# Cross attention in another order: the next pair's scores and the last pair's output ahead of a pair's values

## What is computed

```python
def reference(...):
    x = x + 0.5 * _L0_ffn_ref(_layernorm(x), ...)      # x: (4, 2048, 256)
    x = x + _L0_attn_ref(_layernorm(x), ...)
    x = x + 0.5 * _L0_ffn_ref(_layernorm(x), ...)
    return x

def _L0_attn_ref(hidden_states, Wq, Wk, Wv, Wo, W1, b1, W2, b2):
    initial = hidden_states[:, :256]
    remaining = hidden_states[:, 256:]
    comp = relu(initial @ W1 + b1) @ W2 + b2
    comp = comp.reshape(B, 64, 4, D).mean(axis=2)       # 64 keys
    remaining_out = _cross_attn(remaining, comp, Wq, Wk, Wv, Wo)
    initial_out = _causal_self_attn(initial, Wq, Wk, Wv, Wo)
    return concatenate([initial_out, remaining_out], axis=1)

def _cross_attn(seq, ctx, Wq, Wk, Wv, Wo):              # 16 heads of 16
    scores = einsum('bqhd,bkhd->bhqk', Q, K) * scale
    probs = softmax(scores, axis=-1)
    out = einsum('bhqk,bkhd->bqhd', probs, V).reshape(B, S, 256)
    return out @ Wo
```

## Time and profile before

| | |
|---|---|
| median of 3 runs | 1761.8 us (1752.37 to 1766.24) |
| profiled execution, span | 1859.2 us |
| mean granted clock of TensorE | 0.876 of 2.4 GHz |
| TensorE, busy | 1470.4 us, 79% |
| VectorE, busy | 1063.1 us, 57% |
| ScalarE, busy | 614.9 us, 33% |
| GpSimd, busy | 842.1 us, 45% |

### The profile page before, as it was taken

The page is one execution under the profiler, slowest core; times in us unless marked ns, Lnnn a source line. Parts: engine busy times, 40 slices in busy tenths (PEclk is TensorE's granted clock), DMA queues, the critical chain, the costliest instruction groups (busy, mean ns, idle before and its releaser), DMA issues. The chain is left out here.

```text
span 1859.2 us, 35672 instructions
## 1 busy us (share of the span) xinstructions
PE 1470.4 (79%) x11274; PEld 1241.7 (67%) x11275; DVE 1063.1 (57%) x3355; ACT 614.9 (33%) x1254; POOL 842.1 (45%) x1060
## 2 busy tenths in 40 slices
PE   3988976999987889788787889699783649699760
PEld 3888876988875558655685668588552439598650
DVE  4688745644436676757765775243654666473332
ACT  2333312444433333243223332244331213244220
POOL 4545795555553200221183007655424535656636
PEclk9999987999997999899887989799777769799785
DMA  3643323556553113312231022356423551365555
GB/s 110 197 142 110 99 72 103 167 162 154 162 158 111 46 61 97 111 38 69 69 118 59 24 75 72 112 166 159 137 71 95 159 164 58 108 156 168 159 163 181
DMA packets 175219, 215.72 MB, mean 116 GB/s; under 512 B 18800, under 2 KB 156144, under 8 KB 175088
## 3 DMA queue, kind: packets, MB, share of 16 engines
q0 software_dynamic: 28416, 77.63, 16.3%
q1 hardware_dynamic: 100976, 92.32, 15.6%
q10 hardware_dynamic: 45696, 44.05, 7.3%
HBM read 119.56 MB, written 94.37 MB: 115 GB/s over the span
## 5 line engine op out<-in xcount | busy, mean ns | idle before, releaser
L778 POOL DMA_INDIRECT rows_and_results<-normalised_by_token,rows_of_slots x336 | 319.6, 951 | 227.8 <-PE bank L1608 143.2
L718 POOL DMA_INDIRECT gathered_results<-slot_results,slot x128 | 122.2, 955 | 301.4 <-DVE combined_rows L1447 229.6
L1388 DVE TENSOR_TENSOR rows_transposed_low<-bank,rows_transposed_high 128x512 fp32r<-128x512 f32 x168 | 116.0, 691 | 245.2 <-ACT rows_transposed_high L897 174.7
L1619 PE MATMUL bank<-expert_gate_up_high,rows_transposed_high 128*128 x672 | 212.9, 317 | 29.8 <-DVE rows_transposed_low L1388 14.8
L1620 PE MATMUL bank<-expert_gate_up_low,rows_transposed_high 128*128 x672 | 196.0, 292 | 3.6 <-issue 3.3
L1621 PE MATMUL bank<-expert_gate_up_high,rows_transposed_low 128*128 x672 | 194.7, 290 | 0.0
L1775 PE MATMUL bank<-expert_down,hidden_work 128*128 x672 | 187.8, 404 | 2.8 <-DVE hidden_work L1404 2.3
L793 POOL TENSOR_SCALAR keys_high<-iota,place_in_page_of_choice 128x128 fp32r<-128x128 f32 x96 | 57.7, 601 | 288.2 <-issue 225.2
L1619 PEld LDWEIGHTS bank<-expert_gate_up_high,rows_transposed_high 128*128 128x128 f32 x672 | 133.9, 199 | 46.3 <-issue 44.7
L1619 PE MATMUL bank<-rows_transposed_high,shared_gate_up_high 128*128 128x256 f32 x512 | 160.9, 314 | 1.1 <-DVE hidden_work L1121 1.1
L1620 PE MATMUL bank<-rows_transposed_low,shared_gate_up_high 128*128 128x256 f32 x512 | 154.5, 302 | 0.0
(11 more groups left out here) (275 smaller groups left out, 3700.3 us busy)
## 6 DMA issues: line engine op xcount, KB each, us to landing
slot_results<-rows_and_results ACTq DMA_DIRECT2D x168, 256.0 KB
partial_sums<-rows_and_results SPq DMA_DIRECT2D x96, 256.0 KB, 2.1
rows_and_results<-partial_sums SPq DMA_DIRECT2D x72, 256.0 KB, 2.7
normalised_by_token<-normalised_rows SPq DMA_DIRECT2D x64, 256.0 KB, 3.2
rows_and_results<-in_L_attn_hidden_states SPq DMA_DIRECT2D x32, 256.0 KB, 3.1
normalised_rows<-partial_sums SPq DMA_DIRECT2D x24, 256.0 KB
out<-normalised_rows SPq DMA_DIRECT2D x24, 256.0 KB
rows_and_results<-normalised_by_token,rows_of_slots POOLq DMA_INDIRECT x336
```

Of the source, the lines that this page charges most:

```text
L718: gp.indirect_dma_start(into[:, t, k, :], None, ys[part], bass.IndirectOffsetOnAxis(ap=slot[:, b, k, 2 * i + t:2 * i + t + 1], axis=0))\
L778: gp.indirect_dma_start(rows[:, i % NS, t, :], None, norm_d, bass.IndirectOffsetOnAxis(ap=listed[:, page:page + 1], axis=0))\
L1388: dve.tensor_tensor(flat(xt_l[:, k]), bank[k][:], flat(xt_h[:, k]).bitcast(F32), ALU.subtract)\
L1619: pe.matmul(out_, lh, rh, start=first, stop=False)
```

## The change

In each turn of the loop, TensorE now does the turn of the maxima and the turned scores of i, the rows of i+2, then the output of pair i-1 (before: i-2, at the turn's begin), the scores of i+1, the values of i, and the queries of i+2 at the end (before: i+1, ahead of the maxima). The queries of pair 2 stand ahead of the loop, which is the same place as before. VectorE adds pair i-1 behind the low part of the queries (before: i-2, behind the maxima). ScalarE copies the maxima ahead of the queries. All outputs but that of pair 7 go to bank 1, which holds the queries too: so the output waits for the low part of the queries of the pair two ahead of it, and queries from pair 3 on wait for the addition of the pair three back. The turn of the maxima no longer waits for an addition.

```diff
         def output_bank(ph, i):
-            return bank[int(i == PB - 2 and ph["opens"] is not None)]
+            return bank[int(i < PB - 1)]
...
                 for i in range(1, PB):
-                    if i + 1 < PB:
-                        queries_high(i + 1)
                     if i == PB - 1 and ph["opens"]:
                         token_apply(ph["opens"], 0)
                         token_apply(ph["opens"], 1)
                     maxima(i)
+                    if i + 1 < PB:
+                        queries_high(i + 1)
                     exps(i)
...
                 for i in range(1, PB):
                     maxima(i)
-                    if i > 1:
-                        add(i - 2)
                     norm(i - 1)
                     if i + 1 < PB:
                         queries_low(i + 1)
+                    add(i - 1)
                     if i + 2 < PB:
                         low(i + 2)
...
-                add(PB - 2)
                 norm(PB - 1)
...
                 rows_turned(ph, 2)
+                queries(ph, 2)
                 for i in range(1, PB):
-                    if i > 1:
-                        output(ph, i - 2)
-                    if i + 1 < PB:
-                        queries(ph, i + 1)
                     turn_maxima(ph["a"] + i)
                     scores_turned(ph, i)
                     if i + 2 < PB:
                         rows_turned(ph, i + 2)
+                    output(ph, i - 1)
                     if i == PB - 1 and ph["opens"]:
                         token_turn(ph["opens"], 0)
-                    values(ph, i)
                     if i + 1 < PB:
                         scores(ph, i + 1)
-                output(ph, PB - 2)
+                    values(ph, i)
+                    if i + 2 < PB:
+                        queries(ph, i + 2)
...
                 pe.wait_ge(a_ql.sem, a_ql.freed(a, 1))
+                if i > 2:
+                    pe.wait_ge(a_out.sem, a_out.done(a - 3))
...
                 pe.wait_ge(a_norm.sem, a_norm.done(a))
-                if i + 3 < PB:
-                    pe.wait_ge(a_low.sem, a_low.done(a + 3))
+                if i + 2 < PB:
+                    pe.wait_ge(a_ql.sem, a_ql.done(a + 2))
...
                     pe.wait_ge(x_mx.sem, x_mx.done(a - a // PB - 1))
-                    pe.wait_ge(a_out.sem, a_out.freed(a, 2))
```

## The result

The changed kernel takes 1767.3 us (median of 20 runs, 1758.67 to 1777.6), the kernel before 1760.1 beside it (20 runs, 1752.37 to 1768.64). The ratio of paired runs is 1.004, with a 95% interval of 1.0022 to 1.0057: 4 to 10 us slower. That is within 1%, in the range, and 4 us above the point. The direction is that of the small loss in the sum (+1.5), and the loss is larger than the sum had it.

The account below looks back on a forecast made before the run. Bound: the chain between TensorE, VectorE and ScalarE in the attention stages; TensorE's gain is given back by VectorE's wait for the output. Bounds -2 and +5, middle +1.5: 1761.8 + 1.5 = 1763 us, range 1746 to 1777.

Parts of the forecast that it names:

- the small loss in the sum: Three attention stages at -2 to +5 us, batch 3's stage at 0; middle +1.5, so 1761.8 becomes 1763.
- The case: Whole kernel: nothing measurable changes, chance 0.78, own range 1752 to 1773 us; 0.82 for staying within 1%.
- Neither rival: Faster, VectorE not held: 1744 us, chance 0.13. Slower, TensorE at 1.2 GHz in each pair: 1784 us, chance 0.09.
- The plain pair: A pair without extra VectorE work, such as pair 5: 8.9 us, before 9.88.
- TensorE's loop: Scores 0.60, values 2.45, queries 1.75, turn to exp 1.93, exps 2.07, handing over 0.1: 8.90 us per plain pair.
- scores within 0.2 of the last exp's end: Mark of a right prediction: in the new timeline the next scores start within 0.2 us of the last exp's end.
- The pairs with more work: Pairs where VectorE also combines, does layer norm or statistics: pair 2 11.1, pair 3 14.0, pair 6 12.3 us.
- The tail: Stage end, from pair 7's maxima to the last addition: 17.49 us before, 16.8 at full clock, 18.4 at low clock.
- the pause at pair 7: TensorE waits 4.6 us for pair 7's maxima, before 1.84; low clock assumed behind it, tail 0.9 longer.
- the base: Stage 1 of the one profiled execution before, 83.03 us, taken for all three attention stages.
- the middle of the bounds: Three attention stages together: bounds -2 and +5 us, their middle +1.5 taken as the forecast change.
- the faster rival: Additions don't stall VectorE, so all six gaps gain 1.0: 6 us per stage, 18 in three, 1744; chance 0.13.

Follow-up runs that it names:

- e1: The kernel before, unchanged, profiled once more beside the changed kernel: 1771.51 us in the one run, span 1769.8.
- e5: Changed kernel plus eleven unread matmuls on TensorE ahead of the turn of the maxima of pairs 4 and 7: 1766.1 us, ratio to before 1.0017.
- e3: Changed kernel with VectorE's addition of pair i-2 back directly behind the maxima, TensorE keeping the new order: 1787.1 us, ratio to before 1.0128.
- e4: Changed kernel with VectorE's combining, statistics and low part of the rows put ahead of the addition: 1750.9 us, ratio to before 0.9936.
- e8: Changed kernel with VectorE's other work ahead of the addition, plus six and eight unread matmuls at pairs 4 and 7: 1743.4 us, ratio to before 0.9891.

## Why the prediction was right, and where it was not

**The case and the sign were right.** The main forecast was that the time does not move by more than about 1%, because VectorE's wait for the output gives back what TensorE's chain gains. It held. Neither rival came: VectorE was held at every addition (18.5 us in the stage), so the gain of 18 us is not there; the clock did not fall in the plain pairs 1 and 5, which take 8.90 to 8.91 in all three stages. From the maxima of pair 1 to those of pair 7 it is 66.0 to 66.2, well within the 3 us around 65.5 that the prediction allowed, and the stage of batch 3 is not clearly shorter (134.6 against 134.5 and 135.2).

**The plain pair: 8.9 forecast, 8.91 measured, but partly for a wrong reason.** I had TensorE's loop at 8.90 and VectorE's at 8.69, and took the first as the bound. It is the other way round: two errors, one in each sum, left the number right, and that is luck.

- TensorE's terms were too large. The values with all exps ready take 1.86 (642.65 to 644.51), not 2.45; I had scaled 24 of 32 passes that themselves waited for exps. The queries take 1.53 (644.51 to 646.04), not 1.75, and from turn to exp it is 1.73 (646.04 to 647.77), not 1.93. So that loop sums to 7.9.
- VectorE's had one term too small: from the queries' low part to the addition it is 642.15 - 639.32 = 2.83, where the sum had 0.60 + 2.0. The 0.23 between them is the time from the low part's end to the output's start (640.15). The loop is 2.39 (maxima) + 2.48 (norm) + 2.83 + 0.61 (addition) + 0.60 (low part) = 8.91, the whole distance.
- The mark "scores within 0.2 of the last exp's end" failed accordingly: the exps end at 640.94, and the scores start at 642.05, 1.1 later. The output stands between them on TensorE's queue, and it waited 0.72 for the queries' low part. I had put the output beside the exps, but it is VectorE that sets its start.

The timeline behind the turn, from which 1.73 comes:

```profile
646.04 0.38 PE L1606 MATMUL bank<-identity,score_maxima 128*128 128x128 f32 x2
...
647.77 2.07 ACT L971 ACTIVATE raw_weights<-bank 128x512 f32<-128x512 f32 x4 [0.45 <-PE bank L1917]
```

**The pairs with more work were right in kind, each 0.2 too short.** Pair 2: 11.1 forecast, 11.27 measured. Pair 3: 14.0, and 14.18 and 14.19 in stages 2 and 3 (15.26 in stage 1, with its slow output). Against the 14.46 of its base the prediction took pair 3 for a gain; against the 13.5 to 13.8 of e1 it is a loss. Pair 6: 12.3, and 12.54. The mis-sized 2.6 that is 2.83 is the same in each of them. Pair 4: 10.4, and 10.26 and 10.22 (9.30 in stage 1, where the clock was rising again when the output began, which took 1.98, against 2.94 in stage 2). The maxima of pairs 6 and 7, timeline of VectorE after:

```profile
643.36 2.47 DVE L1486 TENSOR_REDUCE score_maxima<-bank 128x8 f32<-128x512 f32 x4
...
655.90 2.48 DVE L1486 TENSOR_REDUCE score_maxima<-bank 128x8 f32<-128x512 f32 x4
```

**The tail and the clock were right.** 4.6 forecast for the pause at pair 7, 4.95 measured; the clock fell, and the tail is 17.60, 18.15 and 18.13, between the 16.8 at full and the 18.4 at low clock. In e5, with the pauses filled, it is 17.02, so that the fall costs 0.6 to 1.1 here, and at pair 4 the 9.3 to 10.3 become 8.92. The Trainium skill (TensorE: Matmul & The Clock Gate, "HAM oscillation — how this bites in real kernels") says that a pause inside a loop brings the half rate back each time; the windows agree, with 0.50 and 0.55 behind the two long pauses in after and 1.00 in e5. The pause of 2.05 at pair 3 had no forecast, and it cost 1.1 in one stage of three.

**The shared bank was costed by its waits, and they are there.** TensorE stands for 0.30 to 1.30 ahead of five outputs until the queries' low part is done (3.6 in the stage), and e3 shows the other side of it, 1.46 to 6.56 ahead of the queries. Not all of this is the price of the bank: the output waits for the norm in any case, whose last operation ends only some 0.6 ahead of the low part. The Trainium skill (Perfetto Trace Analysis, "Matmuls") has the rule that independent groups rotate through PSUM banks, and the trace agrees, by these numbers. No run has the output in a bank of its own, so what a third bank would give stays open.

**The size of the difference: +1.5 forecast, 4 to 10 measured.** For a stage I forecast 83.03 + 1.0 = 84.0, and the three are 83.79, 84.22 and 84.15. The term that was wrong was the base: the first stage of the profiled execution had one distance of 14.46 that is 13.46 in e1, and the three stages of e1 average 82.2, not 83.0. I had then also taken 1.5 us off by choosing the middle of the bounds, -2 and +5, instead of the sum of three times 1.0 that my own choice of the low clock gave (+3). The traces have 4.0 (against the first profile) and 5.5 (against e1).

**"I find nothing of VectorE's to put there" was the step that failed most.** With this sentence the prediction argued against the faster rival. For the change as it was written that is true, since the code put the low part, the combining and the statistics behind the addition. But e4 shows that they need not stand there. With the order of three calls changed on VectorE the three stages take 17.8 us less than in e1, which is the rival's 18; the whole kernel shows 0.6% of it, some 11 us, and the traces do not say where the rest went.

## What to carry to other kernels

When an instruction on an in-order engine moves to a place where it waits, what is queued behind it pays, so the work that does not need the awaited result belongs ahead of it: here that order alone made the difference between 0.4% slower and 0.6% faster. A loop through two engines has one sum for each; when they come within a few per cent of one another, measure every term in the new arrangement before naming the bound, and take more than one stage as the base. A pause of TensorE costs twice, once as a wait and once in the slower stretch behind it, and where the wait can't be removed, matmuls without a reader can keep the clock, as in e5 and e8, if they end about when the awaited data comes.

## What the runs showed of the hardware

- Filling the pauses with matmuls held the granted clock at 1.00, where it was 0.50 and 0.55 behind idle pauses of 4.98 and 4.95. The 22 records took 5.01, 0.23 each, and the turn behind them started at once.
- A pause of 2.05 at the same place of three stages was followed by a granted clock of 0.63 in stage 1 and of 1.00 in stages 2 and 3; the output took 3.03 in the first and 1.97 in the others.
- The values of a pair, 32 records with 32 weight columns each, ran in 1.86 us with their operands ready, 24% less than the 2.45 that their rate behind the exps had let me expect.
- What remains open: why ScalarE began the exps of pair 3 about 1.0 later in two stages of one execution of the kernel before (1.93 and 1.95 idle against 0.94), why the clock fell behind the pause of 2.05 in one stage only, why the whole time of e4 gains less than its stages, and why the stage of batch 3 spreads over 129 to 139 us.
